# Key/value projections of two cross attentions in a seven-product Strassen form, with the head halves outside the batch loop

## The chip, the cores and the metric

One Trainium2 chip; the kernel runs on one of its cores as one program. The metric is the device time of an execution in microseconds (us); the median of three executions of the kernel before is 1511.18 us. The engines are TensorE (PE in the profile, its weight loads PEld), VectorE (DVE), ScalarE (ACT), GpSimd (POOL) and SyncE (SP, which here only issues DMAs).

## The reference

Six sublayers on x (8 batches x 32 tokens x 512). The first and the fourth are cross attentions, each with its own weights; the change is in these two. What they compute, shortened:

```python
x = x + L0_xattn(layernorm(x), ctx)      # L0: keys = context and latents, no mask
x = x + L0_attn(...); x = x + L0_ffn(...)
x = x + L1_xattn(layernorm(x), ctx, mask)  # L1: keys = context only
x = x + L1_attn(...); x = x + L1_ffn(...)

def xattn(lat, ctx, Wq, Wk, Wv, Wo):      # 32 query heads, 8 kv heads, head_dim 128
    kv = concat([ctx, lat], 1)            # L0: 512 + 32 keys; L1: the 512 of ctx
    q = rms_norm(lat @ Wq)                # 32 tokens a batch
    k = rms_norm(kv @ Wk)                 # ctx: 8 x 512 tokens, 512 -> 1024 columns
    v = kv @ Wv                           # the same, 512 -> 1024 columns
    p = softmax(q @ k.T / sqrt(128))
    return (p @ v) @ Wo
```

## The kernel before, in words

All large products are made three times in fp32r: every operand is split into a high part (rounded, made by ScalarE) and a low part (the rest, made by VectorE as a difference), and `mm3` multiplies high x low, high x high and low x high into the same PSUM bank.

A cross attention has a stage `queries` (layer norm, query projections, and in L0 the keys and values of the latents) and a stage `attend`. In `attend` the work is cut into 16 **units** (`UNITS`): 8 batches b, and inside each batch two halves hf of the kv heads (4 heads, 512 columns). A unit has four **steps** k, one for each tile of 128 context tokens. A step makes 12 matmuls of 128x512 into a `kbank` (`project(k, hf, ...)`: 4 pieces of the contraction of 512, times 3) and 12 into `vbank`. Interleaved with this projection runs the attention of the unit before, one kv head (4 query heads x 32 tokens = 128 rows) in each step. `a` numbers these heads. On TensorE the order of a step is: K product, `pv(a-1)`, `score(a)`, V product, `kt(n)` (four transposes of the normalised keys), `p_transpose(a)`.

The other engines follow, each in an order of its own that is written out by hand in `step` of `scalar`, `vector`, `gpsimd` and `sync`; they are in-order queues, and semaphores with counts tie them together. In each step:

- ScalarE: square of the K bank, `exponential` (exp of the scores, then the division by the row sum), copy of the V bank to `v`, `place_k` (high part of the turned keys), `tail_heads` (L0 only: high part of the turned probabilities of the latent keys), and the high part of a context tile (`context.make_hi`) in half of the steps.
- VectorE: sum of squares, `maximum` of the scores, normalisation of the keys to `kn`, `inverse_sum`, `ot_place`, `lo_of_k`, `pt_copy` (in L0 it ends with the low part of the turned latent probabilities), and the low part of a context tile.
- GpSimd: mean and reciprocal root of the sums of squares (`ms`, `rstd`), and once a unit the split of the queries, in L0 that of the latent keys too.
- SyncE: context tiles of 256 KB, 32 in a layer, each loaded and split once and used for both halves; the rows of the latents' values.

All four column blocks of a layer's key/value weights (K and V, two halves, 8 pieces of 1024 columns to split) stay in SBUF, high and low. The first unit of a layer has no attention beside it. After the last unit `finish` runs the attention of that unit between the 16 parts of the output projection, whose weights were loaded into the place of the key/value weights; its first splits are spread over the steps of the last unit.

## Time and profile before

| | |
|---|---|
| runs, us | 1509.8, 1511.18, 1514.25 (median 1511.18) |
| span of the profiled execution, us | 1508.9 (the page gives no other time for it; the median is 2.3 more than this span) |
| TensorE busy | 1490.3 us, 99% |
| VectorE, ScalarE, GpSimd busy | 876.7, 733.5, 311.5 us (58%, 49%, 21%) |
| DMA | 99.37 MB, mean 66 GB/s |
| chain that ended last | 94% of it TensorE |

The span is the time from the first to the last instruction of one execution. Busy time counts an engine's own instructions; matmuls are pipelined, so that the duration of one (0.39 us for 128x512) is longer than the distance to the next. Distances are read from the start times.

### The profile page before, as it was taken

Reading aid. Unit: us, or ns where it says so; the run is one execution under the profiler, and the core shown is the slowest. Engines: PE = TensorE matmul, PEld = TensorE weight load, DVE = VectorE, ACT = ScalarE, POOL = GpSimd, SP = SyncE. Lnnn points to the kernel's source line nnn. Section 1 sums busy time; section 2 is a strip of 40 time slices with the busy share of each in tenths; the row PEclk is TensorE's granted clock in tenths of the full one; section 3 lists DMA queues with packets and bytes.
Section 4 is the critical chain, followed back from the end, with each engine's and each line's share of the span. In section 5 each row is a group of like instructions: output and inputs, shape, how many; then the busy total and the mean of one; then the engine's idle time right before and its main releaser. Section 6 shows DMA issues by size and latency. Waiting matters only on the chain.

```text
span 1508.9 us, 23714 instructions
## 1 busy us (share of the span) xinstructions
PE 1490.3 (99%) x8326; PEld 1269.7 (84%) x8326; DVE 876.7 (58%) x1645; ACT 733.5 (49%) x1360; POOL 311.5 (21%) x494
## 2 busy tenths in 40 slices
PE   8999999999999999999999999999999999999998
PEld 6888888888888888889778888888888888887887
DVE  6845554555555455758667555455554545577665
ACT  5634444545445454646456444444444444563443
POOL 2322221212222121014233222212222222101000
PEclk9999999999999999999999999999999999999999
DMA  8110000000000001447071000000000000252242
GB/s 326 53 66 30 17 27 19 19 26 12 35 16 26 19 20 62 147 170 258 29 279 60 22 8 28 7 21 21 7 28 7 21 14 15 93 187 91 85 167 98
DMA packets 29306, 99.37 MB, mean 66 GB/s; under 512 B 7040, under 2 KB 7808, under 8 KB 23648
## 3 DMA queue, kind: packets, MB, share of 16 engines
q1 hardware_dynamic: 29248, 98.60, 18.3%
q8 instruction: 36, 0.59, 0.2%
q14 instruction: 22, 0.18, 0.0%
HBM read 95.83 MB, written 2.75 MB: 65 GB/s over the span
## 4 chain that ended last, share of the span: by engine, by line
PE 94%; DVE 3%; ACT 1%; issue 1%; POOL 0%; DMA 0%; SPq 0%; DVEq 0%; POOLq 0%; ACTq 0%
PE g_kbanks L54 10%; PE g_kbanks L56 10%; PE g_kbanks L55 10%; PE g_vbank L54 9%; PE g_vbank L55 9%; PE g_vbank L56 9%; PE g_pobanks L1490 7%; PE g_pobanks L1478 4%; PE g_ktbank L1502 4%; PE g_sbank L1468 3%; PE g_sbank L54 2%; PE g_sbank L56 2%; PE g_sbank L55 2%; PE g_pobanks L54 1%; PE g_pobanks L56 1%; PE g_pobanks L55 1%
## 5 line engine op out<-in xcount | busy, mean ns | idle before, releaser
L54 PE MATMUL g_kbanks<-c_wkv_lo_r,c_cT_hi 128*128 128x512 f32 x640 | 262.5, 410 | 1.9 <-DVE c_wkv_lo_r L339 1.0
L56 PE MATMUL g_kbanks<-c_wkv_hi,c_cT_lo_r 128*128 128x512 f32 x640 | 250.4, 391 | 0.0
L55 PE MATMUL g_kbanks<-c_wkv_hi,c_cT_hi 128*128 128x512 f32 x640 | 249.8, 390 | 0.0
L54 PE MATMUL g_vbank<-c_wkv_lo_r,c_cT_hi 128*128 128x512 f32 x512 | 200.4, 391 | 0.0
L55 PE MATMUL g_vbank<-c_wkv_hi,c_cT_hi 128*128 128x512 f32 x512 | 200.0, 391 | 0.0
L56 PE MATMUL g_vbank<-c_wkv_hi,c_cT_lo_r 128*128 128x512 f32 x512 | 199.8, 390 | 0.0
L56 PEld LDWEIGHTS g_kbanks<-c_wkv_hi,c_cT_lo_r 128*128 128x128 f32 x640 | 120.1, 188 | 26.4
L54 PEld LDWEIGHTS g_kbanks<-c_wkv_lo_r,c_cT_hi 128*128 128x128 f32 x640 | 120.5, 188 | 24.7 <-issue 3.8
L55 PEld LDWEIGHTS g_kbanks<-c_wkv_hi,c_cT_hi 128*128 128x128 f32 x640 | 120.8, 189 | 20.7
L56 PEld LDWEIGHTS g_vbank<-c_wkv_hi,c_cT_lo_r 128*128 128x128 f32 x512 | 96.1, 188 | 20.6
L54 PEld LDWEIGHTS g_vbank<-c_wkv_lo_r,c_cT_hi 128*128 128x128 f32 x512 | 96.2, 188 | 18.5
L55 PEld LDWEIGHTS g_vbank<-c_wkv_hi,c_cT_hi 128*128 128x128 f32 x512 | 96.1, 188 | 17.9
L1680 DVE TENSOR_TENSOR g_stage_r<-g_ktbank,c0a_kT_hi 128x512 fp32r<-128x512 f32 x64 | 44.2, 691 | 110.5 <-ACT c0a_kT_hi L1589 110.5
L1600 ACT ACTIVATE c0a_p<-g_sbank,c0a_nmax 128x544 f32<-128x544 f32 x64 | 45.9, 717 | 125.5 <-DVE c0a_nmax L1691 125.5
L1680 DVE TENSOR_TENSOR g_stage_r<-g_ktbank,c1a_kT_hi 128x512 fp32r<-128x512 f32 x64 | 44.2, 691 | 104.5 <-ACT c1a_kT_hi L1589 104.5
L1600 ACT ACTIVATE c1a_p<-c1a_sm,c1a_nmax 128x512 f32<-128x512 f32 x64 | 46.4, 726 | 118.8 <-DVE c1a_nmax L1694 118.8
L1621 ACT ACTIVATE c1a_sq<-g_kbanks 128x512 f32<-128x512 f32 x64 | 38.2, 597 | 135.7 <-PE g_kbanks L56 135.7
L1730 DVE TENSOR_REDUCE c1a_ss<-c1a_sq 128x4 f32<-128x512 f32 x64 | 43.9, 686 | 89.8 <-ACT c1a_sq L1621 89.7
L1621 ACT ACTIVATE c0a_sq<-g_kbanks 128x512 f32<-128x512 f32 x64 | 38.3, 598 | 118.8 <-PE g_kbanks L56 118.8
L1424 POOL TENSOR_TENSOR c0a_ms<-c0a_ss,c_const 128x4 f32<-128x4 f32 x64 | 12.7, 199 | 401.2 <-DVE c0a_ss L1730 401.2
L1730 DVE TENSOR_REDUCE c0a_ss<-c0a_sq 128x4 f32<-128x512 f32 x64 | 43.9, 686 | 87.3 <-ACT c0a_sq L1621 87.3
L1424 POOL TENSOR_TENSOR c1a_ms<-c1a_ss,c_const 128x4 f32<-128x4 f32 x64 | 12.7, 199 | 384.6 <-DVE c1a_ss L1730 384.6
(538 smaller groups left out, 3562.1 us busy)
## 6 DMA issues: line engine op xcount, KB each, us to landing
c_cT_lo<-in_ctx SPq DMA_DIRECT2D x64, 256.0 KB, 2.5
c_wkv_lo<-in_l_wo SPq DMA_DIRECT2D x16, 1024.0 KB, 4.8
g_stage<-in_l_wq SPq DMA_DIRECT2D x15, 1024.0 KB, 5.2
e_stage<-in_e_w SPq DMA_DIRECT2D x20, 768.0 KB, 4.1
...
```

The costliest lines, as they stand in the source:

```text
L54: nc.tensor.matmul(out, a[0], b[1], start=start, stop=False)
L55: nc.tensor.matmul(out, a[0], b[0], start=False, stop=False)
L56: return nc.tensor.matmul(out, a[1], b[0], start=False, stop=stop)
L1424: nc.gpsimd.tensor_tensor(ms[:, k % 2, :], ss[:, k % 2, :], const[:, 1, :], ALU.add).then_inc(k_mean, 1)
L1468: last = nc.tensor.matmul(bank[:, side * CTX:side * CTX + HALF], q[qp][:, ahf, k, :], kT[kp][:, ahf, k, side * HALF:(side + 1) * HALF], st ...
L1478: last = nc.tensor.transpose(bank[:, t * P:(t + 1) * P], p[:, k % 2, t * P:(t + 1) * P], ident[:])
L1490: last = nc.tensor.matmul(bank[:, 0:P], v[:, ahf, t, k * HD:(k + 1) * HD], pT[:, k % 2, t, :], start=(t == 0), stop=(t == CT - 1 and not t ...
L1502: last = nc.tensor.transpose(ktbank[:, h * P:(h + 1) * P], kn[:, kb, h * P:(h + 1) * P], ident[:])
L1600: nc.scalar.activation(dst, src, ACT.Exp, bias=nmax[:, k:k + 1], scale=1.0 if mask is None else -1.0, accum_out=rsum[:, k:k + 1]).then_inc ...
L1621: nc.scalar.activation(sq[:], kbank[k % 2], ACT.Square, scale=HD ** -0.5).then_inc(k_squared, 1)
L1680: nc.vector.tensor_tensor(kT[1][:, kb, :, kk * P:(kk + 1) * P], ktbank[:, :].rearrange("p (h n) -> p h n", h=UNIT_H), as_f32(kT[0][:, kb, ...
L1730: nc.vector.tensor_reduce(ss[:, k % 2, :], sq[:, :].rearrange("p (h d) -> p h d", h=UNIT_H), AX.X, ALU.add).then_inc(k_summed, 1)
```

## The change

The unit of projection becomes a **pair**: two token tiles (256 tokens) and one half of the heads. The product of a pair is a 2x2 by 2x2 block product: rows are the two token tiles, the contraction of 512 is cut in two, and the columns are K (512) and V (512). Before, the eight block products took 8 x 6 matmuls; now it is seven (7 x 6), of sums and differences of blocks. The new `quad` (one pair) takes the place of two `step`s.

- Context: seven blocks of 256 columns for each pair (`A11, A12, S2, S1, S3, A22, S4`). In the first half of L0 GpSimd makes the sums (`context.sums`, four operations), ScalarE and VectorE split all seven (pieces of 768 and 1024 columns), and SyncE stores both parts in HBM (`store`, 2 x 1792 columns x 128 rows of 4 bytes, 1.8 MB a pair). The second half of L0 and all of L1 `fetch` them from there, with nothing to split.
- Weights: seven blocks of 1024 columns, one half of the heads at a time. The head halves become the outer loop, batches the inner. In the middle of each layer (`is_at(m, PAIRS // 2 - 1)`) the blocks of the other half are loaded, summed by GpSimd (`turned_sum`) and split again (`turned_hi`, `turned_lo`).
- Banks: three products accumulate in one bank whose value is copied out between them (`p1_kept`, `u2_kept`, `u3_kept` on ScalarE); three additions on VectorE (`ka_added`, `vb_added`, `va_added`) finish the other blocks. The next product into the bank waits for the copy.
- L0's latents: their keys and values are projected with weight tiles that come through the stream of the query weights (12 tiles in place of 8); the keys go to HBM and come back 64 KB at a time.
- The first splits of the output weights now lie in the last pair (`last`); the self attention's key weights and tables are loaded later; regions of SBUF are laid out anew.

The core of the diff, with the lines that set the order on the engines:

```diff
 def tensor(pe):
-            for k in range(CT):
-                project(k, hf, kbank[k % 2]).then_inc(k_proj, 1)
-                pv(a - 1, ...)
-                score(a, sbank, ahf, k)
-                project(k, 2 + hf, vbank).then_inc(v_proj, 1)
-                kt(n, k % 2)
-                p_transpose(k, ptbank, sbank)
+            need(pe, ka_added, m)
+            product(side, context.A11, kvw.B11, x_bank, True).then_inc(products, 1)
+            if lags(u, side):
+                pv(a - 1, 1 - par if side else par, (2 * side - 1) % UNIT_H)
+            need(pe, k_normed, 2 * m)
+            product(side, context.A12, kvw.B21, y_bank, True).then_inc(products, 1)
+                kt(2 * m - 1, 1, a if on else 0)
+            pe.wait_ge(p1_kept, m + 1)
+            product(side, context.S2, kvw.T2, x_bank, False).then_inc(products, 1)
+            need(pe, va_added, m)
+            product(side, context.S1, kvw.T1, zbank, True).then_inc(products, 1)
+                score(a, 1 - par, 2 * side)
+            pe.wait_ge(u2_kept, m + 1)
+            product(side, context.S3, kvw.T3, x_bank, False).then_inc(products, 1)
+            if on:
+                kt(2 * m, 0, a)
+                score(a + 1, 1 - par, 2 * side + 1)
+            pe.wait_ge(u3_kept, m + 1)
+            product(side, context.A22, kvw.T4, x_bank, False).then_inc(products, 1)
+            if on:
+                p_transpose(a, 2 * side, 2 * m + 1)
+            pe.wait_ge(vb_added, m + 1)
+            product(side, context.S4, kvw.B22, zbank, False).then_inc(products, 1)
+                pv(a, 1 - par, 2 * side)
+                p_transpose(a + 1, 2 * side + 1, 2 * m + 1)
...
 def scalar(act):
+                tail_heads(a - 1, (2 * side - 1) % UNIT_H)
+            nc.scalar.activation(kn[:, 0, :], x_bank, ACT.Copy).then_inc(p1_kept, 1)
+                place_k(2 * m - 1, ...)
+            square(2 * m, kn[:, 0, :])
+            nc.scalar.activation(v[:, par, 2 * side, :], x_bank, ACT.Copy).then_inc(u2_kept, 1)
+            if prepared(hf, m + 1):
+                for i in range(2):
+                    context.make_hi(act, *following(hf, b, side), i)
+                exponential(a, 2 * side)
+            nc.scalar.activation(v[:, par, 2 * side + 1, :], x_bank, ACT.Copy).then_inc(u3_kept, 1)
+                divide(a, 2 * side)
+            place_k(2 * m, 2 * side, par, u)
+                exponential(a + 1, 2 * side + 1)
+                tail_heads(a, 2 * side)
+            square(2 * m + 1, x_bank)
+                divide(a + 1, 2 * side + 1)
...
 def vector(dve):
+                pt_copy(a - 1, (2 * side - 1) % UNIT_H)
+                normalise(2 * m - 1, 1, y_bank)
+                ot_place(a - 1, ...)
+            nc.vector.tensor_tensor(kn[:, 0, :], y_bank, kn[:, 0, :], ALU.add).then_inc(ka_added, 1)
+                lo_of_k(2 * m - 1, ...)
+            total(2 * m, 0)
+                maximum(a, 2 * side)
+            normalise(2 * m, 0, kn[:, 0, :])
+                inverse_sum(a, 2 * side)
+                context.make_lo(dve, *following(hf, b, side), 0)
+            nc.vector.tensor_tensor(v[...], zbank[:, :], v[...], ALU.add).then_inc(vb_added, 1)
+            lo_of_k(2 * m, 2 * side, par)
+            if is_at(m, PAIRS // 2 - 1):
+                kvw.turned_lo(dve, 0)
+            if last:
+                for i in range(2):
+                    wo.make_lo(dve, i)
+                maximum(a + 1, 2 * side + 1)
+                pt_copy(a, 2 * side)
+                inverse_sum(a + 1, 2 * side + 1)
+            if is_at(m, PAIRS // 2 - 1):
+                kvw.turned_lo(dve, 1)
+            total(2 * m + 1, 1)
+            nc.vector.tensor_tensor(v[...], zbank[:, :], v[...], ALU.add).then_inc(va_added, 1)
+                context.make_lo(dve, *following(hf, b, side), 1)
+                ot_place(a, u - 1, 2 * side)
+            if is_at(m, PAIRS // 2 - 1):
+                for n in range(2, kvw.COUNT):
+                    kvw.turned_lo(dve, n)
...
 def gpsimd(pool):
+            if prepared(hf, m + 1):
+                context.sums(pool, *following(hf, b, side))
+            split_queries(u, par, 2 * m)     # side 1; holds root(2 * m, 0)
+            latent_keys(u, par)              # side 1, L0
+            root(2 * m, 0)                   # side 0
+                kvw.turned_sum(pool, 0)      # 1 and 2 behind it, 3 behind the root
+            root(2 * m + 1, 1)
...
 def sync(sp):
+                    sp.wait_ge(context.stored, 16 * m + 16)
+                    sp.wait_ge(products, made(m, "p2"))
+                    context.load(sp, nb, side, 0)
+                    sp.wait_ge(products, made(m, "p4"))
+                    context.load(sp, nb, side, 1)
+                else:
+                    sp.wait_ge(products, made(m, "p6"))
+                    context.fetch(sp, nb, side, 0)
+                    sp.wait_ge(products, made(m, "p3"))
+                    context.fetch(sp, nb, side, 1)
+            if prepared(hf, m + 1):
+                context.store(sp, *following(hf, b, side))
```

## Rows read from the trace of the kernel before

**Rows 1.** The page: span, busy time and share, and the granted TensorE clock in 40 slices

```profile
span 1508.9 us, 23714 instructions
...
PE 1490.3 (99%) x8326; PEld 1269.7 (84%) x8326; DVE 876.7 (58%) x1645; ACT 733.5 (49%) x1360; POOL 311.5 (21%) x494
...
PEclk9999999999999999999999999999999999999999
```

**Rows 2.** Windows inside L0's and L1's attention: length, busy of PE, PEld, DVE, ACT, POOL

```profile
300.00:620.00 320.00, 319.60 (x1859) 278.33 (x1858) 173.81 (x334) 159.06 (x335) 67.44 (x111) 1.00 0.10 35
...
900.00:1300.00 400.00, 400.00 (x2171) 342.72 (x2170) 200.97 (x482) 177.06 (x330) 85.37 (x128) 1.00 0.06 21
```

**Rows 3.** Timeline of PE, one L0 step: start, duration, engine, line, what, count

```profile
400.93 0.48 PE L54 MATMUL g_kbanks<-c_wkv_lo_r,c_cT_hi 128*128 128x512 f32 x1
...
405.52 0.40 PE L54 MATMUL g_vbank<-c_wkv_lo_r,c_cT_hi 128*128 128x512 f32 x1
...
408.29 0.60 PE L1502 MATMUL g_ktbank<-g_ident,c0a_kn 128*128 128x128 f32 x4
...
409.19 0.48 PE L54 MATMUL g_kbanks<-c_wkv_lo_r,c_cT_hi 128*128 128x512 f32 x1
```

**Rows 4.** Timeline of PE, one L1 step

```profile
1006.82 0.48 PE L54 MATMUL g_kbanks<-c_wkv_lo_r,c_cT_hi 128*128 128x512 f32 x1
...
1009.64 1.05 PE L1490 MATMUL g_pobanks<-c1a_pT,c1a_v 128*128 128x128 f32 x8
...
1010.45 0.48 PE L54 MATMUL g_sbank<-g_stage_r,c1a_q_hi 128*128 128x512 f32 x1
...
1011.23 0.39 PE L54 MATMUL g_vbank<-c_wkv_lo_r,c_cT_hi 128*128 128x512 f32 x1
...
1013.96 0.60 PE L1502 MATMUL g_ktbank<-g_ident,c1a_kn 128*128 128x128 f32 x4
...
1014.75 0.47 PE L54 MATMUL g_kbanks<-c_wkv_lo_r,c_cT_hi 128*128 128x512 f32 x1
```

**Rows 5.** Timeline of ACT and DVE around the same L0 step

```profile
406.48 0.72 ACT L1600 ACTIVATE c0a_p<-g_sbank,c0a_nmax 128x544 f32<-128x544 f32 x1 [1.92 <-DVE c0a_nmax L1691]
...
407.52 0.75 ACT L1603 ACTIVATE c0a_p<-c0a_p,c0a_rinv 128x544 f32<-128x544 f32 x1 [0.23 <-DVE c0a_rinv L1687]
408.48 0.60 ACT L1630 ACTIVATE c0a_v<-g_vbank 128x512 f32<-128x512 f32 x1 [0.21 <-PE g_vbank L56]
408.98 0.59 ACT L1589 ACTIVATE c0a_kT_hi<-g_ktbank 128x512 fp32r<-128x512 f32 x1
409.47 0.56 ACT L1612 ACTIVATE c0a_pT_stack<-g_sbank 32x128 fp32r<-32x128 f32 x2
...
405.72 0.72 DVE L1691 TENSOR_REDUCE c0a_nmax<-g_sbank 128x1 f32<-128x544 f32 x1 [0.45 <-PE g_sbank L1468]
406.68 0.69 DVE L1746 TENSOR_TENSOR c0a_kn<-g_kbanks,c0a_rstd 128x512 f32<-128x512 f32 x1 [0.23 <-POOL c0a_rstd L1427]
...
409.60 0.69 DVE L1680 TENSOR_TENSOR g_stage_r<-g_ktbank,c0a_kT_hi 128x512 fp32r<-128x512 f32 x1 [1.87 <-ACT c0a_kT_hi L1589]
410.21 0.68 DVE L1701 COPY c0a_pT<-g_pobanks 128x512 f32<-128x512 f32 x1
410.91 0.28 DVE L1705 TENSOR_TENSOR c0a_pT_stack<-g_sbank,c0a_pT_stack 32x128 fp32r<-32x128 f32 x1
```

**Rows 6.** Timeline of POOL in L0: the wide query split of a unit

```profile
414.87 1.29 POOL L1430 TENSOR_TENSOR c0a_q_lo<-c_qT,c0a_q_hi 128x512 fp32r<-128x512 f32 x1
```

**Rows 7.** Timeline of DVE and PE: transposes that had to wait for normalised keys, unit 1

```profile
118.42 0.69 DVE L1746 TENSOR_TENSOR c0a_kn<-g_kbanks,c0a_rstd 128x512 f32<-128x512 f32 x1 [0.86 <-POOL c0a_rstd L1427]
...
119.17 0.66 PE L1502 MATMUL g_ktbank<-g_ident,c0a_kn 128*128 128x128 f32 x4
```

**Rows 8.** Timeline of the query stage: a 1024-column weight split on DVE beside POOL

```profile
67.70 1.01 POOL L532 TENSOR_TENSOR c0q_rstd<-c0q_ms,c_const 128x4 f32<-128x4 f32 x1
...
68.12 1.23 DVE L202 TENSOR_TENSOR c_wkv_lo_r<-c_wkv_lo,c_wkv_hi 128x1024 fp32r<-128x1024 f32 x1 [0.24 <-ACT c_wkv_hi L197]
```

More of the change, by code:

```diff
@@ L205, in wait_column, with half, low, load @@
-    def wait_column(self, pe, col):
-        pe.wait_ge(self.lo_ready, self.HALVES * (self.order.index(col) + 1))
-    def column(self, col):
-        return tuple(h[:, col, :] for h in self.split)
+    def half(self, hf, i):
+        col, at = (hf, i) if i < 2 else (2 + hf, i - 2)
+        return self.src[col][:, at * self.WIDTH:(at + 1) * self.WIDTH]
+    def low(self, block):
+        return self.raw[:, block, 1, :]
+    def load(self, sp, hf, i, place):
+        sp.dma_start(place, self.half(hf, i)).then_inc(self.loaded[i], 16)
@@ L533, in gpsimd @@
                                     ALU.pow).then_inc(rstd_ready, 1)
+            if n in SUM_AT:
+                kvw.first_sum(pool, SUM_AT.index(n))
+            if NL and n == CTX_SUM_AT:
+                context.sums(pool, 0, 0)
+        for n in range(NN, OUTPUTS):
+            if n in SUM_AT:
+                kvw.first_sum(pool, SUM_AT.index(n))
     def tensor(pe):
@@ L1451, in gpsimd, with product @@
             moe.constants(pool)
-        run(pool, step, finish)
+        run(pool, quad, finish)
     def tensor(pe):
-        def project(k, col, bank):
-            for c in range(DC):
-                a = tuple(h[:, k, c * P:(c + 1) * P] for h in context.split)
-                last = mm3(nc, bank[:, :], a, tuple(h[:, c * UW:(c + 1) * UW] for h in kvw.column(col)),
-                           c == 0, c == DC - 1)
+        def product(side, left, right, bank, start):
+            a, wt = context.block(side, left), kvw.block(right)
+            for c in range(DC // 2):
+                last = mm3(nc, bank[:, :], tuple(h[:, c * P:(c + 1) * P] for h in a),
+                           tuple(h[:, c * UW:(c + 1) * UW] for h in wt),
+                           start and c == 0, c == DC // 2 - 1, not start)
@@ L1572, in finish @@
-            out.product(pe, 2 * UNIT_H + 1)
-            for q in range(2 * UNIT_H + 2, PARTS):
-                out.product(pe, q)
-                if after is not None and q == PARTS - 2:
+                score(a, 1, j)
+                if j:
+                    pv(a - 1, 1, j - 1)
+                out.product(pe, 2 * j + 2)
+                p_transpose(a, j, 2 * m)
+                out.product(pe, 2 * j + 3)
+            pv(LAST + UNIT_H - 1, 1, UNIT_H - 1)
+            for i in range(2 * UNIT_H + 2, PARTS):
+                out.product(pe, i)
+                if after is not None and i == PARTS - 2:
@@ L1792, in finish @@
[L1792 to L1796 removed]
+                if after is not None and j == 1:
+                    after.kv_split_lo(dve)
+            out.make_lo(dve, 11)
+            for i in range(14, 16):
+                wo.make_lo(dve, i)
+            ot_place(LAST + UNIT_H - 1, UNITS - 1, UNIT_H - 1)
+            out.make_lo(dve, 12)
@@ L1797, in finish @@
+            for i in range(12, PARTS):
+                if i + 1 < PARTS:
+                    out.make_lo(dve, i + 1)
+                if after is not None and i < PARTS - 1:
+                    after.wide_lo(dve, i - 12)
                 if then:
-                    then[0].early_lo(dve, q - 12)
+                    then[0].early_lo(dve, i - 12)
             out.add(dve, 0)
@@ L2459 @@
 KV_BYTES = 4 * 2 * 4 * DC * UW
-ZONE_BYTES = 60672
+ZONE_BYTES = 60288
 REST_BYTES = 8768
```

1077 lines of the change are left out of this document (626 added, 451 removed).

## The prediction

> **What bounds the kernel now.** I read the page first: of a span of 1508.9 us TensorE is busy 99%, at full clock in all 40 slices [rows 1]. The reader is to see that nothing else can be the bound on average: VectorE is at 58%, ScalarE at 49%. The windows inside the two attentions say the same of the stage that changes: 0.4 us of idle TensorE in 320 us of L0, none in 400 us of L1 [rows 2]. So matmuls taken away come back as time, as long as nothing takes their place. How much one is worth is not its duration but the distance of the starts: 12 matmuls take 408.29 - 405.52 = 2.77 us in L0, 0.231 each [rows 3], and 1013.96 - 1011.23 = 2.73 in L1, 0.227 each [rows 4]. Behind fp32 transposes a product takes some 0.08 more (1006.82 to 1009.64: 2.82) [rows 4]. A step is 409.19 - 400.93 = 8.26 us in L0 and 1014.75 - 1006.82 = 7.93 in L1 [rows 3, 4]; a pair of tiles 16.52 and 15.86.
>
> **What the change removes.** 48 matmuls a pair become 42: 6 x 0.231 = 1.39 us in L0, 1.36 in L1. There are 32 pairs a layer, so 32 x (1.39 + 1.36) = 88 us, 5.8% of the time. That is the ceiling; one more change from transposes to a product in each pair costs 0.08 of it and is about repaid: eight transposes take 1014.75 - 1013.96 = 0.79 [rows 4], which I part as 0.43 for four ahead of others and 0.36 for four ahead of a product, and both groups of keys now stand ahead of a product or a score.
>
> **What it adds on the path.** A step before has two products, each 2.8 us, and almost any answer of the other engines fits beside one. A pair now has seven of 1.36 to 1.39 us, with copies and additions between them, and four queues in a fixed order. I walked one pair through these queues with durations of the rows: a 512-column operation takes ScalarE 0.60 (0.50 to the next start), VectorE 0.69 (0.61), exp 0.72 and 0.19 for its sum, division 0.75, latent heads 0.56, their low part 0.28 [rows 5]; `rstd` 1.01 and `ms` (taken at 0.3 with its wait) on GpSimd [rows 8]; a hand-over 0.04, to TensorE 0.06 (118.42 + 0.69 to 119.17) [rows 7], for which I take 0.12, since the transposes then run 0.06 longer. Matmul results come 0.16 after the next one may start.
>
> The walk in L1, from the start of p1: p1 1.44, pv 2.25, p2 3.69, transposes 4.05, p6 5.49, p5 6.85, score(a) 7.63, p7 8.99. VectorE meanwhile: the scores are there at 7.78, `maximum` to 8.50, and only behind it in the queue the normalisation of tile 2m, 8.50 to 9.19. TensorE wants to turn these keys at 8.99 and starts at 9.31: **stall one, 0.32**. Then transposes 9.67, score(a+1) 10.45, p4 11.81, p_transpose(a) 12.17, p3 13.61, pv(a) 14.42. The second softmax: exp(a) 8.60 to 9.40, u3 copy 9.90, division 10.55, high keys 11.14, low keys on VectorE 11.79, `maximum` 12.47, exp(a+1) 12.57 to 13.37, square 13.87, division 14.59. TensorE starts p_transpose(a+1) at 14.71: **stall two, 0.29**. The next pair starts at 15.07. Saved: 15.86 - 15.07 = 0.79 of 1.36.
>
> L0, second half (blocks fetched, nothing split): stall one is 0.30. Between exp(a+1) and pv(a) stand the latent heads: ScalarE makes tail_heads(a) behind exp(a+1), to 14.07, and VectorE's low part ends at 14.39; pv(a) is wanted at 13.97 and starts at 14.51, **0.53**. With 0.03 more a pair is 15.96, saved 0.56 of 1.39.
>
> L0, first half: VectorE also splits 768 + 1024 columns a pair. By the slope from 0.69 at 512 [rows 5] to 1.23 at 1024 [rows 8] that is 0.96 + 1.22. The second piece stands ahead of ot_place and pt_copy(a-1) of the next pair, so that pv(a-1) comes **1.03** late: 16.99, which is 0.47 *more* than before. All stalls lie in one circle (score, maximum, exp, copy, division, keys, maximum, exp, heads, pv, score), so none is absorbed by the next.
>
> **Once a layer.** The first unit has no attention: before, two steps are 11.8; its pairs come to 11.2 and 13.3 (p2 of the second waits 1.7 us for the keys of the first: square, sum, GpSimd 1.3, normalisation). Cost 1 us a layer. The turn to the other half: 7 low parts of 1.23 on VectorE, 7 high ones of about 1.05 on ScalarE, and four sums of 1024 columns on GpSimd, which I take at 2.4 (512 columns take 1.29 [rows 6]), with the last behind `root(2m+1)`. Two low parts fall into the pair, delaying it by 1.5; five stand ahead of pt_copy and the normalisation of the next pair, whose pv starts at 8.2 in place of 1.4: 6.8 to 7.2 us. If the loads or sums came later still, the same place would grow. The last pair of a layer has 4 output-weight and 2 head splits in one place: 2.6.
>
> **The sum.** L0: 13 pairs (2 to 14) x 0.47 = +6.1; pair 15 +2.0; pair 16 23.1 - 16.5 = +6.6; 15 x -0.56 = -8.4; last pair +2.6, first unit +0.9: +9.8. L1: 28 x -0.79 = -22.1; pair 15 +0.7, pair 16 +6.0, last +2.6, first unit +1.0: -11.8. Together -2. To this +3 for what has no row: four weight blocks split late in the first pair, a busier query stage (its TensorE work is the same: 24 outputs in L0, 16 in L1), one more turn of keys in each `finish`. Bounds for it 0 and +8: hidden as the splits before are, or 4 splits of 1.23 and 3 us of an output each exposed once. So 1508.9 + 1 = 1510 as a span; the median of the runs is 2.3 more: **1512**. In this case I count the turned parts, late context and klat transfers as hidden: a raw load or fetch has one to two pairs (15 to 30 us) for 0.5 to 1.8 MB, and the loads before moved 99.37 MB without a wait of TensorE's in these windows [rows 2].
>
> With hand-overs of 0.02 in the walk (0.05 to TensorE) the sum falls by 11; with 0.07 (0.25), or with no overlap of consecutive operations (0.69 and 0.60 between starts), it rises by 17 to 19. The walk's own range is 1498 to 1532.
>
> **Rivals.** (1) *The saving comes through.* If the queues run further ahead than I think (scores early enough that stalls one and two vanish), only the once-a-layer terms stay: 1511 - 88 + 25 = 1448; with half the stalls, 1480. For it: average loads are low, VectorE's would be 11.6 of 17 us in the fullest pair. Against: the circle is a chain of dependences, not a load. 0.18. (2) *Slower: GpSimd and VectorE stand in each other's way.* Normalisation of tile 2m now reads both inputs from SBUF and meets the query split (1.29 us [rows 6]) in every second pair: 0.3 x 30 = 9; the context split meets `rstd` in the first half of L0, 0.8 x 14 = 11. 1512 + 20 = 1532; it decides over 0.1 us a pair. Against it: the weight split at 68.12 starts inside `rstd` (67.70 to 68.71) and takes its usual 1.23 [rows 8]. The Trainium skill, "SBUF — State Buffer", section "Who interferes with whom", says that a Vector instruction with two SBUF inputs and a GpSimd one that reads SBUF exclude each other for the whole instruction; by that rule rival 2 is the forecast, and the row, small as its GpSimd operand is, does not bear it out. 0.12. (3) *The turn or the HBM path is late.* Each first-half pair waits in SyncE's queue for its 1.8 MB store before it may load; 1 us late a pair is 13, and a turn 5 us longer is 10: 1525 to 1535. 0.10. (4) *The clock falls* behind stalls of 7 us at the turns. It is 1.0 in all slices, and beside short stalls in unit 1 too [rows 1, 7]; a few us at 1.2 GHz in place of 2.4 would cost as much again. Inside (3). The walk itself has 0.60: 0.16 of it faster by over 0.3% (4.5 us, about what a measurement can tell from no change), 0.22 within, 0.22 slower.
>
> **How the numbers follow.** Faster 0.18 + 0.16 = 0.34; same 0.22; slower 0.12 + 0.10 + 0.22 = 0.44. Likeliest 1512. The range leaves out the full saving below and the worst of rivals 2 and 3 above: 1474 to 1537.
>
> **What would show it.** 42 product matmuls a pair; periods of 17.0, 16.0 and 15.1 us between starts of p1; TensorE's waits led by the transposes on `kn`, then pv on the low part of the latent heads and p_transpose on the division; TensorE idle around 100 us in place of 19 (1508.9 - 1490.3 [rows 1]); a hole of 7 us in the middle of each attention. Wrong if `kn` isn't waited for (rival 1), if VectorE's operations grow in duration (rival 2), or if TensorE waits for DMAs (rival 3).

## The result and the profile after

The changed kernel takes 1541.97 us (median of four runs, 1540.7 to 1542.61), the kernel before 1510.49 beside it: ratio 1.0204, 95% interval 1.0189 to 1.0218. It is slower by 31.5 us; 1512 was predicted, with a range of 1474 to 1537. In the profiled executions the spans are 1540.8 and 1508.9. Of the ten executions of e11 below one took 3791.93 us, the other nine 1507.12 to 1508.82; its ratio goes by the nine.

The page of the changed kernel, its lines for [rows 1] and the chain:

```profile
span 1540.8 us, 23740 instructions
...
PE 1448.2 (94%) x7942; PEld 1191.0 (77%) x7942; DVE 1043.0 (68%) x1829; ACT 764.1 (50%) x1412; POOL 422.8 (27%) x574
...
PEclk9999999998999999999999999999899999999999
...
DMA packets 65516, 215.13 MB, mean 140 GB/s; under 512 B 16976, under 2 KB 21840, under 8 KB 58160
...
PE 63%; DVE 16%; issue 9%; ACT 5%; DMA 4%; POOL 3%; SPq 0%; DVEq 0%; ACTq 0%; POOLq 0%
```

The two attention windows, as [rows 2]:

```profile
300.00:620.00 320.00, 302.66 (x1725) 250.20 (x1724) 209.61 (x377) 160.84 (x339) 94.44 (x128) 0.98 0.41 134
900.00:1300.00 400.00, 382.77 (x2049) 318.26 (x2048) 255.69 (x543) 174.92 (x338) 95.18 (x131) 0.98 0.38 123
```

TensorE issues 384 matmuls less and is busy for 42 us less, but it is idle for 93 us in place of 19, and the clock is below full in both windows. The 384 matmuls were worth 88 us by the distance of their starts, so what remains is busy for 46 us longer; part of that is waiting that does not show as idle time (see e9 and e12). TensorE's waits:

```profile
PE g_pobanks L1712 <- DVE c0a_pT_stack L1994: 23.1, 20, 9.4
PE g_pobanks L1712 <- DVE c1a_pT L1990: 11.8, 4, 7.2
PE g_ktbank L1725 <- DVE c1a_kn L2012: 9.2, 30, 0.5
PE g_kbanks L54 <- ACT c0a_v L1899: 5.0, 2, 4.2
PE g_ktbank L1725 <- DVE c0a_kn L2012: 4.3, 15, 0.4
```

The columns are sum, number and longest. A wait of 0.3 in 30 pairs and one of 9.4 at one place look alike in a sum; the last column parts them. The steady pairs (all but the first two, the two at the turn and the last) are nearly as walked. ScalarE's copy of p1 marks a pair; two neighbouring ones in L0's first half, L0's second half and L1:

```profile
193.05 0.60 ACT L1879 ACTIVATE c0a_kn<-g_kbanks 128x512 f32<-128x512 f32 x1 [0.84 <-PE g_kbanks L56]
210.01 0.60 ACT L1879 ACTIVATE c0a_kn<-g_kbanks 128x512 f32<-128x512 f32 x1 [0.93 <-PE g_kbanks L56]
...
454.61 0.60 ACT L1879 ACTIVATE c0a_kn<-g_kbanks 128x512 f32<-128x512 f32 x1 [0.93 <-PE g_kbanks L56]
470.41 0.60 ACT L1879 ACTIVATE c0a_kn<-g_kbanks 128x512 f32<-128x512 f32 x1 [0.84 <-PE g_kbanks L56]
...
1206.80 0.60 ACT L1879 ACTIVATE c1a_kn<-g_kbanks 128x512 f32<-128x512 f32 x1 [2.27 <-PE g_kbanks L56]
1222.00 0.60 ACT L1879 ACTIVATE c1a_kn<-g_kbanks 128x512 f32<-128x512 f32 x1 [2.67 <-PE g_kbanks L56]
```

That is 16.96, 15.80 and 15.20; the means are 16.9, 15.9 and 15.1, predicted 17.0, 16.0 and 15.1. Laid out by place, from the starts of p1 and of the first row of each stage, against the same places of the kernel before (its pairs take 16.5 and 15.85 on average):

| place | predicted, us | measured, us |
|---|---|---|
| steady pairs: L0 2 to 14, 17 to 30; L1 27 pairs | +6.1, -7.8, -21.3 | +5.0, -8.5, -19.3 |
| pairs 15 and 16, L0 and L1 | +8.6, +6.7 | +12.8, +13.3 |
| first unit, L0 and L1 | +0.9, +1.0 | +8.9, +1.3 |
| last pair and finish, L0 and L1 | +2.0, +1.8 | +5.8, +5.9 |
| query stages L0 and L1, other | +3 | +3.0, +3.5, +0.3 |
| sum | +1 | +32 (spans: +31.9) |

The sum of the steady pairs agrees (-22.9 for -23.0); 31 us are lost at places that come once a layer.

**The turn in L1.** VectorE, GpSimd and TensorE at the same moment:

```profile
1089.28 7.90 DVE L212 TENSOR_TENSOR c_wkv_r<-c_wkv,c_wkv_r 128x1024 fp32r<-128x1024 f32 x5
1097.10 0.68 DVE L1990 COPY c1a_pT<-g_pobanks 128x512 f32<-128x512 f32 x1
...
1089.96 2.73 POOL L206 TENSOR_TENSOR c_wkv<-c_wkv 128x1024 f32<-128x1024 f32 x1
...
1090.20 0.40 PE L56 MATMUL g_kbanks<-c_wkv_r,c_cT_r 128*128 128x512 f32 x1
1097.83 2.08 PE L1712 MATMUL g_pobanks<-c1a_pT,c1a_v 128*128 128x128 f32 x8 [7.23 <-DVE c1a_pT L1990]
1099.56 0.77 PE L54 MATMUL g_kbanks<-c_wkv_r,c_cT_r 128*128 128x512 f32 x1
1100.13 0.63 PE L55 MATMUL g_kbanks<-c_wkv_r,c_cT_r 128*128 128x512 f32 x1
1100.56 0.63 PE L56 MATMUL g_kbanks<-c_wkv_r,c_cT_r 128*128 128x512 f32 x1
```

and the window behind the hole, as [rows 2]:

```profile
1097.80:1103.00 5.20, 5.17 (x19) 4.48 (x19) 1.29 (x3) 0.00 (x0) 0.00 (x0) 0.50 0.00 0
```

Five low parts stand ahead of pt_copy, as predicted; but they take 7.90 (8.04 in L0) and not 5 x 1.15 = 5.75 (1.23 each, less 0.08 of overlap): the last GpSimd sum runs beside them, and one of them waits for it. Behind the hole the products are 0.43 apart, with a granted clock of 0.50 (1.2 GHz) for 5.2 us.

The pair before, 15, loses time in the same way. Its first low part starts 0.07 behind a sum and takes 3.41 for 1.22, and pv(a) waits 2.56 for the pt_copy behind it:

```profile
1081.19 2.40 POOL L206 TENSOR_TENSOR c_wkv<-c_wkv 128x1024 f32<-128x1024 f32 x1 [0.17 <-POOL c_wkv L206]
1081.26 3.41 DVE L212 TENSOR_TENSOR c_wkv_r<-c_wkv,c_wkv_r 128x1024 fp32r<-128x1024 f32 x1 [0.25 <-ACT c_wkv_r L209]
...
1085.95 1.50 PE L1712 MATMUL g_pobanks<-c1a_pT,c1a_v 128*128 128x128 f32 x8 [2.56 <-DVE c1a_pT L1990]
```

In L1 pairs 15 and 16 take 18.85 and 26.12 us (+3.0 and +10.3; +0.7 and +6.0 predicted), in L0 18.83 and 27.00 (+2.3 and +10.5; +2.0 and +6.6 predicted).

**The first unit of L0.** SyncE's queue and TensorE:

```profile
101.82 0.42 SPq L415 DMA_DIRECT2D ctx_split_dram<-c_cT_r  x1
107.64 0.83 SPq L384 DMA_DIRECT2D c_cT<-in_ctx  x2
...
118.32 0.80 PE L54 MATMUL g_kbanks<-c_wkv_r,c_cT_r 128*128 128x512 f32 x1 [4.19 <-ACT c0a_v L1899]
```

```profile
114.00:126.00 12.00, 7.81 (x23) 5.60 (x22) 5.96 (x7) 3.44 (x5) 8.95 (x13) 0.72 0.24 84
```

The raw load of pair 2 is issued only when the store of pair 0 has landed; the store stands behind the latents' transfers. GpSimd's sums, ScalarE's high parts, and behind those in its queue the copy `u3_kept`, are what TensorE waits 4.2 us for, and the clock is 0.72 in these 12 us (0.50 from 118 to 124).

**The query stage in L1.**

```profile
833.35 4.55 DVE L161 TENSOR_TENSOR c1q_w_lo<-g_stage,c1q_w_hi 128x1024 fp32r<-128x1024 f32 x2
...
833.93 2.89 POOL L206 TENSOR_TENSOR c_wkv<-c_wkv 128x1024 f32<-128x1024 f32 x1
...
845.23 0.66 PE L600 MATMUL g_pobanks<-g_ident,c1q_xn 128*128 128x128 f32 x4 [1.98 <-DVE c1q_xn L833]
```

Two low parts take 4.55 in place of 2.4, beside a sum of GpSimd's; 9 us later VectorE's first low part of the key/value weights waits 1.70 for the last sum, and TensorE for the queries' normalisation that stands behind it.

### The profile page after: what moved, and what is told of

Read it like the earlier page. It is cut to its first block, busy times and chain, and to the rows that moved or that the text cites. A ratio compares the mean times of both kernels' runs of the same rounds, so it can differ in the third digit from the quotient of the medians.

```text
span 1540.8 us, 23740 instructions
## 1 busy us (share of the span) xinstructions
PE 1448.2 (94%) x7942; PEld 1191.0 (77%) x7942; DVE 1043.0 (68%) x1829; ACT 764.1 (50%) x1412; POOL 422.8 (27%) x574
## 4 chain that ended last, share of the span: by engine, by line
PE 63%; DVE 16%; issue 9%; ACT 5%; DMA 4%; POOL 3%; SPq 0%; DVEq 0%; ACTq 0%; POOLq 0%
PE g_kbanks L54 9%; PE g_kbanks L56 8%; PE g_kbanks L55 8%; PE g_pobanks L1712 7%; PE g_ktbank L1725 4%; PE g_vbank L54 4%; PE g_vbank L55 4%; PE g_vbank L56 3%; PE g_pobanks L1700 3%; PE g_sbank L1687 2%; DVE c0a_nmax L1978 2%; DVE c1a_kn L2012 2%; PE g_pobanks L54 1%; PE g_sbank L54 1%; DVE c_cT_r L410 1%
## 5 line engine op out<-in xcount | busy, mean ns | idle before, releaser
L54 PE MATMUL g_kbanks<-c_wkv_r,c_cT_r 128*128 128x512 f32 x768 | 322.5, 420 | 16.3 <-ACT c0a_v L1899 5.0
L56 PE MATMUL g_kbanks<-c_wkv_r,c_cT_r 128*128 128x512 f32 x768 | 304.0, 396 | 0.0
L55 PE MATMUL g_kbanks<-c_wkv_r,c_cT_r 128*128 128x512 f32 x768 | 303.1, 395 | 0.0
L54 PEld LDWEIGHTS g_kbanks<-c_wkv_r,c_cT_r 128*128 128x128 f32 x768 | 146.1, 190 | 45.0 <-DVE c_wkv_r L212 5.3
L56 PEld LDWEIGHTS g_kbanks<-c_wkv_r,c_cT_r 128*128 128x128 f32 x768 | 145.4, 189 | 34.3
L55 PEld LDWEIGHTS g_kbanks<-c_wkv_r,c_cT_r 128*128 128x128 f32 x768 | 146.3, 190 | 21.4
L54 PE MATMUL g_vbank<-c_wkv_r,c_cT_r 128*128 128x512 f32 x256 | 106.8, 417 | 0.6 <-DVE c0a_v L2061 0.6
L56 PE MATMUL g_vbank<-c_wkv_r,c_cT_r 128*128 128x512 f32 x256 | 101.0, 395 | 0.0
L55 PE MATMUL g_vbank<-c_wkv_r,c_cT_r 128*128 128x512 f32 x256 | 100.8, 394 | 0.0
L1712 PEld LDWEIGHTS g_pobanks<-c0a_pT,c0a_v 128*128 128x128 f32 x512 | 64.1, 194 | 45.0 <-DVE c0a_pT_stack L1994 29.2
L1712 PE MATMUL g_pobanks<-c0a_pT,c0a_v 128*128 128x128 f32 x512 | 73.0, 287 | 25.5 <-DVE c0a_pT_stack L1994 23.1
L1835 ACT ACTIVATE c0a_kT_hi<-g_ktbank 128x512 fp32r<-128x512 f32 x64 | 38.2, 597 | 95.8 <-PE g_ktbank L1725 95.8
L1712 PEld LDWEIGHTS g_pobanks<-c1a_pT,c1a_v 128*128 128x128 f32 x512 | 67.4, 194 | 19.0 <-DVE c1a_pT L1990 13.6
L1712 PE MATMUL g_pobanks<-c1a_pT,c1a_v 128*128 128x128 f32 x512 | 69.3, 279 | 11.8 <-DVE c1a_pT L1990 11.8
L1978 DVE TENSOR_REDUCE c0a_nmax<-g_sbank 128x1 f32<-128x544 f32 x64 | 46.0, 719 | 48.8 <-PE g_sbank L1687 48.8
L1611 POOL TENSOR_TENSOR c0a_rstd<-c0a_ms,c_const 128x4 f32<-128x4 f32 x64 | 65.6, 1025 | 5.0
```

The costliest lines, as they stand in the source:

```text
L54: nc.tensor.matmul(out, a[0], b[1], start=start, stop=False, skip_group_check=reopen)
L55: nc.tensor.matmul(out, a[0], b[0], start=False, stop=False, skip_group_check=reopen)
L56: return nc.tensor.matmul(out, a[1], b[0], start=False, stop=stop, skip_group_check=reopen)
L1611: nc.gpsimd.tensor_tensor(rstd[:, k, :], ms[:, k, :], const[:, 0, :], ALU.pow).then_inc(k_rstd, 1)
L1712: last = nc.tensor.matmul(obank[:, 0:P], v[:, apar, t, k * HD:(k + 1) * HD], pT[:, k % 2, t, :], start=(t == 0), stop=(t == CT - 1 and not ...
L1835: nc.scalar.activation(kT[0][:, par, :, kk * P:(kk + 1) * P], ktbank[:, :].rearrange("p (h n) -> p h n", h=UNIT_H), ACT.Copy).then_inc(kt_ ...
```

## The experiments

All are edits of the changed kernel (1541.97 us). Differences are taken to that median; each was timed beside the kernel before, whose medians were 1509.99 to 1510.9. "Steady pairs" are those of the table; their lengths are read from the traces and repeat within a few hundredths of a us.

**e1: without the turn.** The loads, `turned_sum`, `turned_hi` and `turned_lo` are deleted, and

```diff
-        pe.wait_ge(self.lo_ready, (self.TURNED_LO.index(i) + self.COUNT if half else self.FIRST.index(i)) + 1)
+        pe.wait_ge(self.lo_ready, self.FIRST.index(i) + 1)
```

> Leaves out the reload, sums and splits of the weights in the middle of each layer; the second half uses the blocks of the first half (its results are then those of other heads). Theory A (most of the miss sits in once-a-layer places, and the turn is the largest): pairs 15 and 16 fall from 45.8 to about 33 us in L0 and from 45.0 to about 30 in L1, the holes and the half clock behind them go, total -28: 1514. Theory B (the loss is spread: GpSimd and VectorE get in each other's way in all pairs, and what waits at the turn would wait elsewhere): -14 or less, 1528 or more.

1514.57 us, -27.4; ratio to before 1.003 (1.0019 to 1.004). Theory A is right, and the turn is the largest single cost: pairs 15 and 16 fall to 32.5 us in L0 and 30.2 in L1. What is left of the change with no turn at all is still no gain.

**e2: the turn spread.** The low parts 3 to 6 and the high parts 4 to 6 move into pair 16; high part 3 stays in pair 15, and the blocks T3 and T4 change places in the order.

```diff
 def vector(dve):
                 normalise(2 * m - 1, 1, y_bank)
+            if is_at(m, PAIRS // 2):
+                kvw.turned_lo(dve, 3)
...
             if is_at(m, PAIRS // 2 - 1):
-                for n in range(2, kvw.COUNT):
-                    kvw.turned_lo(dve, n)
+                kvw.turned_lo(dve, 2)
```

> Same work, other order at the turn: of the five low parts that stand in one row ahead of pt_copy, four move behind pt_copy and behind the normalisation into the next pair, each just ahead of the product that needs it, with its high part. Theory A (the row of splits in the queue is what pv waits for): by the queue walk 5 us less in each layer, and with the clock that no longer falls to half for 3 and 5 us (1.6 + 2.5) some 14 less: 1528. Rival (the GpSimd sums of 2.4 to 3.2 us and the loads set the end of the turn, not the order): no change, 1542.

1527.2 us, -14.8; ratio 1.0105 (1.0088 to 1.0122). TensorE's wait at pair 16 shrinks from 7.23 to 0.33 in L1 and from 9.43 to 2.60 in L0:

```profile
366.56 2.08 PE L1712 MATMUL g_pobanks<-c0a_pT,c0a_v 128*128 128x128 f32 x8 [2.60 <-DVE c0a_pT_stack L1998]
...
1086.35 1.16 PE L1712 MATMUL g_pobanks<-c1a_pT,c1a_v 128*128 128x128 f32 x8 [0.33 <-DVE c1a_pT L1994]
```

About half of the turn's cost was the order in one queue. Pair 15 keeps its length (18.84 and 18.73 us).

**e3: the hole filled.**

```diff
+            if is_at(m, PAIRS // 2):
+                need(pe, va_added, m)
+                for _ in range(6 if tail else 5):
+                    product(side, context.A11, kvw.B11, zbank, True)
```

> TensorE gets idle work at the turn: six (L0) and five (L1) extra products of 1.4 us into a free bank between the first product of pair 16 and the pv that waits, so that the hole of 9.4 and 7.2 us is filled; they are overwritten. Theory A (the hole costs twice: its length, and a clock of 0.5 for 3.2 us in L0 and 5 us in L1 after it): the granted clock stays 1.0 and the time falls by 1.6 + 2.5 = 4: 1538. Rival (the clock behind the hole costs nothing because another engine is late anyway): 1542. If the products end after the low part that pv waits for, up to 1 us is added back at each.

1538.36 us, -3.6; ratio 1.0181 (1.0164 to 1.0198). The window behind the hole in L1, clock in the third column from the end:

```profile
1098.00:1106.00 8.00, 7.83 (x40) 6.29 (x39) 4.00 (x10) 3.27 (x7) 1.21 (x2) 1.00 0.31 98
```

It is 1.00 in all 8 us, where it was 0.50 for 5.2. Pair 16 is shorter by 1.4 us in L0 and 2.3 in L1. So the fallen clock costs 4 us beside the holes' own 17; 1.1 and 1.6 us of waiting remain, the products were one too few. The extra products stand 0.227 apart. The L1 figure is loose: in traces whose edits do not touch this place (e4, e5, e13, e14) L1's pair 16 takes 24.8 to 26.2 us.

**e4: the second context piece.**

```diff
             nc.vector.tensor_tensor(v[:, par, 2 * side, :], zbank[:, :], ..., ALU.add).then_inc(va_added, 1)
-            if prepared(hf, m + 1):
+            if is_at(m, 0) and prepared(hf, m + 1):
                 context.make_lo(dve, *following(hf, b, side), 1)
...
                     ot_place(a - 1, u - 2, UNIT_H - 1)
+            if not is_at(m, 0) and not is_at(m, 1) and prepared(hf, m):
+                context.make_lo(dve, b, side, 1)
```

> The second piece of the context split on VectorE (1024 columns) moves from before pt_copy to behind ot_place of the next pair, which is the pair that reads it. Theory A (the walk's stall of 1.03 us in each pair of L0's first half is real, and comes from this place in the queue): 13 to 14 pairs x 1.03 = -14: 1528. Theory B (port contention or a transfer sets these pairs at 16.9): -3 or less, 1539 or more; the piece then only moves the wait.

1532.24 us, -9.7; ratio 1.0145 (1.0128 to 1.0162). Pairs 4 to 12 go from about 17.0 to 16.1, by 0.88 and not 1.03. From pair 0 to pair 15 it is 11.6, of which the turn takes back 1.5 (26.3 to 27.8 us for pair 15). The stall was real and of nearly the size walked.

**e5: the store of pair 0 earlier.**

```diff
         if vl is not None:
+            context.store(sp, 0, 0)
             sp.wait_ge(placed, NN)
...
-            if is_at(m, 0) and tail:
-                context.store(sp, 0, 0)
```

> The store of pair 0's split context is issued from the query stage's queue, ahead of the latents' stores, instead of behind them at 101.8. Theory A (in the first unit the raw load of pair 2 waits in SyncE's queue for that store until 107.6, and the sums, high parts and products of pair 1 and 2 wait for it): the load is issued at about 102, the idle 4.2 us at 114.1 goes and the clock beside it stays up, -5 to -6: 1536. Rival (GpSimd's sums of 4 x 1.2 to 1.6 us beside VectorE set the first unit, the load is only the last of several waits): -2 or less, 1540.

1535.36 us, -6.6; ratio 1.0163 (1.0146 to 1.018).

```profile
79.92 0.35 SPq L415 DMA_DIRECT2D ctx_split_dram<-c_cT_r  x1
...
101.96 1.20 SPq L384 DMA_DIRECT2D c_cT<-in_ctx  x2
...
114.89 0.50 PE L54 MATMUL g_kbanks<-c_wkv_r,c_cT_r 128*128 128x512 f32 x1 [0.69 <-ACT c0a_v L1898]
```

Load at 101.96 for 107.64, wait of 0.69 for 4.19, and the clock in 114 to 126 is 1.00. L0's first unit takes 26.9 us in place of 33.0.

**e6: the queries' low part behind the second root.**

```diff
             else:
                 root(2 * m, 0)
...
             root(2 * m + 1, 1)
+            if side == 1:
+                rest()
```

Here `rest()` is the operation that `split_queries` made behind its root.

> GpSimd's low part of the queries (1.28 us) moves from before the normalisation of tile 2m to behind the root of tile 2m+1, so that it no longer runs beside that normalisation. Theory A (the exclusion of GpSimd and VectorE lengthens that operation from 0.69 to 0.9-1.0 in odd pairs, but the pair loses under 0.1 by it): 30 pairs x 0.05 = -1 to -2: 1540. Theory B (the exclusion is a main part of the loss): 15 x 0.3 a layer = -9: 1533.

1540.05 us, -1.9; ratio 1.0192 (1.0175 to 1.0209). The total hides more than it shows. In the changed kernel the normalisation of tile 2m meets the query split in every second pair; two neighbouring pairs of L1:

```profile
1212.69 1.30 POOL L1625 TENSOR_TENSOR c1a_q_lo<-c_qT,c1a_q_hi 128x512 fp32r<-128x512 f32 x1
1213.51 1.03 DVE L2012 TENSOR_TENSOR c1a_kn<-c1a_kn,c1a_rstd 128x512 f32<-128x512 f32 x1
...
1228.91 0.69 DVE L2012 TENSOR_TENSOR c1a_kn<-c1a_kn,c1a_rstd 128x512 f32<-128x512 f32 x1
```

With the edit it takes 0.69 (0.68 in L0) in all steady pairs. L1's steady pairs fall from 15.14 to 14.98 on average (the pairs with a query split by 0.3 each), those of L0's first half from 16.87 to 16.78, those of its second half stay: 5 to 6 us in all. L0's turn takes 2.8 us more, where the query split now stands ahead of the last sum in GpSimd's queue (L1's pair 15 is 1.6 shorter, its pair 16 1.1 longer); the rest of what is given back wasn't traced. So theory A's 0.05 a pair is right for the total and too low for the steady pairs, and theory B's 9 us is too high.

**e7: the normalisation ahead of the maximum.**

```diff
+            normalise(2 * m, 0, kn[:, 0, :])
             if on:
                 maximum(a, 2 * side)
-            normalise(2 * m, 0, kn[:, 0, :])
```

> VectorE normalises tile 2m ahead of the maximum of score(a) instead of behind it. That removes the wait of kt(2m) for the keys (stall one, 0.3 us a pair), but exp(a) and all behind it in the circle come later. Theory A (the queue walk): pairs of 17.4, 16.3 and 15.5 us in place of 17.0, 16.0 and 15.1, together +24: 1566. Rival (each wait counts by itself: without stall one a pair is 0.3 shorter): 60 x 0.3 = -18: 1524.

1588.45 us, +46.5; ratio 1.0517 (1.0499 to 1.0534). The direction is the walk's, the size is twice it. Every second pair shows why; GpSimd and VectorE are both released by one root:

```profile
1218.52 1.29 POOL L1625 TENSOR_TENSOR c1a_q_lo<-c_qT,c1a_q_hi 128x512 fp32r<-128x512 f32 x1
1218.59 1.77 DVE L2012 TENSOR_TENSOR c1a_kn<-c1a_kn,c1a_rstd 128x512 f32<-128x512 f32 x1 [1.40 <-POOL c1a_rstd L1611]
```

GpSimd started 0.07 earlier and ends at 1219.81; VectorE ends 0.55 later. It stood still for 1.77 - 0.69 = 1.08 of the 1.22 us that were left of the other's instruction. By the Trainium skill, "SBUF — State Buffer", section "Who interferes with whom", the one that issues first holds the shared port pair for its whole instruction; this trace agrees but for the last 0.14 us.

**e10: e6 and e7 together.**

> The normalisation ahead of the maximum, and GpSimd's low part of the queries behind the second root. In the run with the first edit alone the normalisation took 1.77 us in place of 0.69 in every second pair, since both were released by the same root. Theory A (the +46 there are about 17 to 24 of the circle and 30 x 1.0 of the exclusion of VectorE and GpSimd): against the run with the query edit alone (1540.1) +17 to +24: 1557 to 1564. Rival (the exclusion is only seen in durations, the order does all of it): +46: 1586.

1564.26 us; ratio 1.0353 (1.0335 to 1.037): +24.2 against e6, +24.2 less than e7. So the +46.5 is 24 of order (the walk gave 24) and 24 of exclusion, less the 1.9 that the exclusion costs in the changed kernel already. Rival 2 is real as a mechanism; the same two instructions cost 0.3 us where `maximum` stands between the root and the normalisation, and 1.08 where one root releases both.

**e8: the weight sums one output earlier.**

```diff
-    SUM_AT = [OUTPUTS - 16 + n for n in (8, 9, 11, 12)]
+    SUM_AT = [OUTPUTS - 16 + n for n in (7, 8, 10, 11)]
```

> The four GpSimd sums of the first half's weights in the query stage are issued one output earlier (all four are what VectorE's first low part waits for, 1.7 us at 840.7 in L1, and TensorE behind it 1.97 at 843.3). Theory A (the last sum is what is late): -1.5 to -2 in L1, 0 to -1 in L0: 1539.5. Rival (each sum excludes VectorE's operations with two inputs in SBUF, 2.2 us at 833 to 838, wherever it stands): no gain, 1542, the idle time only moves.

1537.38 us, -4.6; ratio 1.0177 (1.016 to 1.0194). From the first transposes of L1's queries to its first context product it takes 54.61 us in place of 56.29, L0's first context product comes at 90.32 in place of 91.46; TensorE's 4.2 us before pair 2 shrink to 2.3. More than either theory gave: the sums hold up both layers' query stages and the first unit.

**e9: p5 behind p7.**

```diff
-            product(side, context.S1, kvw.T1, zbank, True).then_inc(products, 1)
             if on:
...
                 score(a, 1 - par, 2 * side)
...
             product(side, context.S3, kvw.T3, x_bank, False).then_inc(products, 1)
+            product(side, context.S1, kvw.T1, zbank, True).then_inc(products, 1)
```

> One product changes its place on TensorE: p5 (S1 x T1 into the V bank) moves from ahead of score(a) to behind p7, so that score(a) and all that hangs on it starts one product (1.4 us) earlier; VectorE's first V addition waits for p5. Nothing else changes. Theory A (the stalls of a pair are one circle, score - maximum - exp - copy - division - keys - maximum - exp - heads - pv - score, so a start 1.4 us earlier takes most of them away): by the queue walk pairs of 16.4, 15.4 and 14.7 us, -19.7 in L0 and -12.0 in L1: 1510. Rival (each wait stands for itself: the keys of tile 2m, the latents' low part, the division): only the wait for the keys shrinks or another grows, -5 or less, 1537.

1533.08 us, -8.9; ratio 1.0139 (1.0122 to 1.0156). Theory A falls in its size. L0's pairs are 16.45 and 15.7, L1's stay at 15.1 where 14.7 was walked. Before and after the edit, the same window of L1:

```profile
1150.00:1300.00 150.00, 147.01 (x796) 122.20 (x795) 94.42 (x210) 65.22 (x129) 33.31 (x50) 1.00 0.37 123
```

```profile
1150.00:1300.00 150.00, 149.08 (x796) 121.56 (x795) 98.55 (x208) 68.01 (x128) 33.23 (x50) 1.00 0.38 123
```

TensorE's idle time falls from 3.0 to 0.9 us, and as many matmuls are done. A matmul's modelled length hides a stall up to 0.16. With p5 gone from between p6 and p7 nothing covers the copy `u2_kept`, and `score(a)` meets the low keys: the row from p6's last matmul to score(a) is 0.50 at its longest, for 0.23. The walk had 0.12 for such hand-overs.

**e11: e2, e4, e5, e6 and e8 together. e12: these and e9.**

> The five edits that helped, together: spread turn (-14.8), context piece moved (-9.7), early store (-6.6), earlier sums (-4.6), queries' low part behind the second root (-1.9). If they act at different places their gains add: 1542.0 - 37.6 = 1504.4. If they are cover for one another (the same idle time counted twice), the sum is 5 to 15 higher: 1510 to 1520.

> The five edits and p5 behind p7. Theory A: with the context piece moved the queue walk gives 19.6 (L0) and 12.0 (L1) less for the moved product, pairs of 15.4, 15.4 and 14.7: 1504 - 32 = 1473, 2.5% below the kernel before. Rival: what limits is then the turn, the ends and other exclusions, half of it: 1488.

e11: 1507.6 us, ratio 0.9978 (0.9968 to 0.9988). The gains add up to 3 us short of their sum. e12: 1504.14 us, ratio 0.9961 (0.9947 to 0.9975): 38 us less than the changed kernel and 0.4% faster than the kernel before. The expected 1473 was far off. Little idle time is left:

```profile
1120.00:1300.00 180.00, 179.15 (x962) 147.42 (x960) 115.00 (x251) 84.08 (x157) 39.91 (x60) 1.00 0.39 129
400.00:560.00 160.00, 159.56 (x923) 134.19 (x922) 104.31 (x194) 81.87 (x173) 38.84 (x62) 1.00 0.39 124
```

TensorE is idle for 0.5% and 0.3%, and a pair still takes 14.98 in L1 and 15.58 in L0's second half, 0.87 and 0.91 below the kernel before. At that the steady pairs are worth 32 x 1.78 = 57 us, not 88. But this is not what is left with every stall gone, since short stalls hide in the modelled length of a matmul. In L1 score(a) waits for the low keys behind p6 (here 0.42 after the last start in place of 0.23):

```profile
1216.74 0.40 PE L56 MATMUL g_kbanks<-c_wkv_r,c_cT_r 128*128 128x512 f32 x1
1217.16 0.50 PE L54 MATMUL g_sbank<-g_stage_r,c1a_q_hi 128*128 128x512 f32 x1
```

p6 to the start of score(a) takes 1.58 on average, where it takes 1.47 when nothing waits, score(a) 0.88 for 0.68 and p7 1.44 for 1.36: 0.4 a pair. Added up from the stretches that nothing holds up, a pair would take 14.58 in L1 and 15.22 in L0's second half, 1.27 less than before in both, some 81 us for 64 pairs. In L1 the moved product took longer waits away and put hidden ones of the same size in their place: e11 has 14.96. And the turn still costs 10.3 us in L0 and 6.4 in L1.

**e13: without the fetches.**

```diff
-                    context.fetch(sp, nb, side, 0)
+                    context.fetch(sp, nb, side, 0, little=not is_at(m, PAIRS // 2 - 1) and not is_at(m, PAIRS // 2 - 2))
```

> In L0's second half and in L1 the fetches of the split context move 8 columns instead of 768 and 1024, except for the first unit of each half; the products then read the blocks of the first unit (the result is that of other batches). Theory C (the transfers into SBUF slow TensorE's reads): the distance of products falls from 0.2304 to 0.2274 in L1 and from 0.233 to 0.229 in L0, 44 pairs x 0.15 = -6.5: 1535.5. Rival (the distance comes from the products themselves, with other weights and banks, or from waits on semaphores): it stays, and the time too: 1542.

1541.48 us, no change; ratio 1.0208 (1.0191 to 1.0225). The window of L1, DMA share in the column before the last:

```profile
1150.00:1300.00 150.00, 147.01 (x797) 122.32 (x796) 94.75 (x210) 65.68 (x129) 32.97 (x49) 1.00 0.02 2
```

DMA share 0.02 in place of 0.37, TensorE's line nearly the same, products 0.2298 apart for 0.2300. The transfers cost nothing in the steady pairs, and theory C falls.

**e14: the output weights' splits later. e15: this in e12.**

```diff
 def vector(dve):
-            if last:
-                for i in range(2):
-                    wo.make_lo(dve, i)
             if on:
                 maximum(a + 1, 2 * side + 1)
                 pt_copy(a, 2 * side)
                 inverse_sum(a + 1, 2 * side + 1)
+            if last:
+                wo.make_lo(dve, 0)
```

The second is at the end of the pair, 2 and 3 behind `lo_of_k` in the finish, ScalarE's high parts likewise.

> In the last pair of a layer the high and low parts of the first output weights move behind exp, latent heads, maximum, pt_copy and division of head a+1; two of the four go to the finish, behind lo_of_k. Theory A (as at the turn: pv waits for pt_copy behind a row of splits, 2.5 us at 626 in L0 with a clock of 0.77 behind it, 1.5 and 0.55 in L1): -5: 1537. Rival (the finish needs these weights at once and gives the time back): 0 to -1, 1541.

> All edits that helped and this one. Theory A: 1504.1 - 5 = 1499. Rival: 1503.

1552.71 us, +10.7; ratio 1.0278 (1.0261 to 1.0295). In e15 1511.19, +7.1 against e12. Both theories miss:

```profile
628.07 1.16 PE L1712 MATMUL g_pobanks<-c0a_pT,c0a_v 128*128 128x128 f32 x8 [0.27 <-DVE c0a_pT_stack L1992]
630.90 0.66 PE L1700 MATMUL g_pobanks<-g_ident,c0a_p 128*128 128x128 f32 x4 [1.61 <-ACT c0a_p L1851]
633.00 0.77 PE L54 MATMUL g_kbanks<-c_wkv_r,c_cT_r 128*128 128x512 f32 x1 [1.33 <-DVE c_wkv_r L471]
```

The wait for pt_copy falls from 2.54 to 0.27, but the high parts now stand ahead of the division, and the finish's first part needs the weights at once: 1.61 + 1.33 lost for 2.27 won. The finish behind it has waits of 1.08 and 1.67 where there were none and 0.68, and clocks of 0.79 to 0.88. This later place is the worse one; others weren't tried.

## Why the prediction was wrong

**Right.** The sum of the steady pairs: -22.9 measured, -23.0 predicted. The stall in L0's first half (e4), the hole in the middle of each attention and its cause (e1, e2), and the wait for `kn` in every pair of L1 (9.2 us over 30). The same walk gave the direction and size of e7 as far as it is order (e10). Rival 1, the saving in full, did not come. Transfers in steady pairs cost nothing (e13).

**The step that failed is "Once a layer"**, where +24 was taken with the "+3 for what has no row", and +55 measured. By term:

- *The turn*, 8.6 and 6.7 predicted, 12.8 and 13.3 measured. The mechanism was the one named, the row of splits ahead of pt_copy; its operations were taken at their length with nothing beside them. `turned_sum` 3 beside the five low parts adds 2.2 us in each layer, and in L1's pair 15 another sum adds 2.2 to a single low part. The clock behind the hole takes some 1.5 and 2.5 (e3: 3.6 together). That accounts for what is missing in L0 (4.2) and in L1 (6.6).
- *The first unit*, 0.9 taken, 8.9 measured in L0. "I count the turned parts, late context and klat transfers as hidden: a raw load or fetch has one to two pairs" is true of every pair but the first, whose store had not yet been issued. e5 gives 6.1 of it by the trace. In L1 (1.3 for 1.0) the walk held.
- *The last pair and the finish*, 3.8 taken, 11.7 measured. Only the pair was walked, the finish was put under "+3 for what has no row". In these stages TensorE is idle for 5.4 us in L0 and 5.5 in L1, before for 1.5 and 0.4; 2.5 and 2.1 of it are a pv behind pt_copy, as walked, the rest short waits for splits, the division and the keys; the mean clock of L0's finish is 0.97. No run takes them apart; e14 shows only that the later place tried for the splits is worse.
- *The query stages*, 6.5 where 3 was taken with the rest; inside its bounds of 0 to 8. e8 shows the GpSimd sums as cause of 4.6, which includes some of the first unit.

**Right in the sum, not in the parts.** The walk of L1 had 14.46 us of work and two stalls, 0.32 and 0.29. By the starts of the rows it is 14.58 of work, a first stall of 0.5 and hardly a second one (pv ahead of p_transpose takes 0.89 where 0.81 was taken). The first is longer because the normalisation is held up by the query split in every second pair, which the walk left to rival 2. In L0's second half the 0.53 predicted at pv(a) is 0.25. TensorE's idle time (100 predicted, 93 measured) agrees by luck: with 88 us of matmuls gone and 100 of idle time the span would be 1502 and not 1541; the rest is slower clock, hidden stalls and wider distances inside busy time.

Products stand 0.230 apart inside a product in L1 and 0.233 in L0, where the kernel before has 0.227 and 0.229 (means over the rows of the windows): 0.13 and 0.17 us a pair, 9 us in all. With it the ceiling of 88 comes down to some 81. Why the products are further apart is open: not the transfers (e13), nor blocks of this kind as such (0.227 in e3's hole, where the other engines split weights in SBUF). In L1 it is the products right behind transposes or pv that stand 0.231 to 0.232 apart, p5 and p7 0.227.

**The rivals.** (4), the clock, was put "inside (3)" at a few us, and measured 3.6 at the turns. (3), late turn and HBM path, gave 1525 to 1535 and named steady waits and the turn; its place was the first unit. (2) was argued down with [rows 8], where a low part beside GpSimd's small `rstd` kept its length. For the big operands, which are what the change adds to GpSimd, the exclusion is nearly full (e7). The row that spoke against it had the wrong size. The price that rival 2 named, 0.3 us in every second pair, is what L1's trace shows, 5 to 6 us over the steady pairs (9 predicted); the steady sum agreed only because another stall was walked too long. At the turns 6.6 us more are this, where TensorE waits for those very rows; in L1's query stage it takes 2.1 of VectorE's time. So at least 6.6 of the 31 us missed are rival 2's, which got a chance of 0.12.
